# Where the transpose of dt·u and the diagonal scalings stand in their queues: a Mamba block with a quantised feed-forward on one Trainium2 core

## The chip, the cores and the metric

The kernel runs on one core of a Trainium2 chip. The metric is the device time of one execution in microseconds (us). The core's engines work from queues of their own and meet through semaphores: PE (TensorE, matrix products and transposes), DVE (VectorE), ACT (ScalarE), POOL (GpSimd) and SP, which issues the DMAs. Each engine takes its instructions strictly in the order in which they were written, and one that waits holds up all behind it.

## The reference, cut to what matters

```python
x = x + tanh(g_x) * mamba(ctx, z=layernorm(x))      # 4 batches, 512 positions, 512 channels, 16 states
x = x + tanh(g_f) * ffn(layernorm(x))               # 512 -> 2048 -> 512, weights ternary, activations in 8 bits
# mamba, per batch: u = silu(conv(ctx @ w_in)); dt = softplus(...); B, C from u @ w_xp
#   state[n] = state[n] * exp(dt * A[n]) + (dt * u) * B[n];   y += state[n] * C[n]      (n = 0..15, along 512 positions)
#   y = (y + D * u) * silu(z)
# ffn: bitlinear(silu(bitlinear(x, w_gate)) * bitlinear(x, w_up), w_down); bitlinear divides by an rms norm,
#   rounds each row to 8 bits, and multiplies by weights rounded to -1, 0, 1
```

## The kernel before, in words

After a first part (convolution, projections, statistics), the work is cut into 16 stages, one for each batch and each 128 channels (batch `s // 4`, channel block `s % 4`). A stage `s` does the 16 state recurrences of its block: ACT makes `exp(dt * A[n])` into one of three PSUM banks (`exponential`, L1090), DVE runs the scan of state `n` (`scan`, L1428), and the states are then multiplied by C, by DVE (`times_c`, L1450, states 2, 3, 6, 7, 10, 14, 15), or by POOL (L833 for four pairs, L847 for state 11, called `alone`). PE transposes each product and adds it up in PSUM (`y_sum`, `y_sum_pooled`, `y_sum_alone`). The term `(dt * u) * B[n]` comes from POOL (L838), but from stage 5 (`PE_FROM`) on, for states 4 and 5, from PE: `du_transpose` (L515) transposes `dt * u` into the bank `pT` by four 128x128 transposes, ACT's `copy_duT` (L1120) takes it to SBUF, and `db_state` (L522) multiplies it by diagonal matrices that hold B of the two states at each position. ACT writes these diagonals once for a batch, by eight instructions `diagonal(b, i, k)` (L1125): state `i` of the two, block `k` of the positions.

From stage 4 on each stage also does the feed-forward of one token tile `t1 = s - 4` (gate, up, silu) and ends that of an earlier one (`t2 = s - 5`: maximum, scale, transposes; the down product in pieces called `fill`). At its four first tiles of a batch (`t1 % 4 == 0`, stages 4, 8, 12) the tile's statistics are made within the stage, which makes these stages longer.

The order on each engine is written out by hand, and ACT's goes by steps `n = 0..15`. At step `n` of stage `s` ACT makes the exponential of state `n + 2` (at steps 14 and 15 those of states 0 and 1 of the next stage), and after it what else belongs to the step: n = 0 `squares(t2)` (L1056); n = 1 `skip`; n = 2 `scale_x` (L1037); n = 3 sums of the next tile; n = 4 `copy_xqT` (L1043), which waits for PE's transpose of the quantised tile (L546); n = 5, 6 `scale_h`; n = 7, 8 `copy_hqT`; n = 11 the four `gate_silu` (L1048) with the loads of another activation table before and after them; n = 14 `z_copy` (L1108), which takes `pT` to SBUF; n = 15 `copy_duT(s + 1)`. The exponential of a state may run when the scan three states before it is done.

PE ends a stage with `up(t1, 2)`, `du_transpose(s + 1)`, `up(t1, 3)`, `y_sum_alone`, `y_sum(s, 14)`, `c_bcast(s, 15)` (L472, which spreads C of state 15 to all partitions for DVE's `times_c`), and begins the next one with `y_sum(s - 1, 15)`. `y_sum_alone` waits for POOL's L850, `y_sum(s, 15)` for DVE's product L1456 of state 15. DVE's order at that turn is: scan of state 0 of the new stage, `times_c` of state 15, scan 1, scan 2, `gated_y` (L1462), scan 3. "Turn" below is this passage from one stage to the next.

Of the kernel before, what the change touches and what calls it, by code (L numbers as in the profile page):

```python
# [19 lines left out]
NT = D // P  # L20
UNITS = BATCH * NT
# [31 lines left out]
PE_FROM = PLAIN + 1  # L53
# [8 lines left out]
def own(s):  # L62
    return [n for n in range(NS) if n // CH not in pooled(s) and not alone(s, n)]
# [18 lines left out]
def pool_pairs(s):  # L82
    return [c for c in range(NCH) if s < PE_FROM or c != PE_PAIR]
# [5 lines left out]
def db_count(s, c):  # L89

    return DB_AT[s] + pool_pairs(s).index(c) + 1


def by_pe(s, n):
# [19 lines left out]
def past(eng, sem, value):  # L114

    if value > 0:
        eng.wait_ge(sem, value)
# [7 lines left out]
def build(nc, x, ctxT, g_x, g_f, w_in, w_conv, b_conv, w_xp, w_dt, b_dt, a_log, d_skip, w_gate, w_up, w_down,  # L125
          bc_rows, u_rows, out):
    with ExitStack() as stack:
# [267 lines left out]
        def _(pe):  # L395
# [76 lines left out]
            def c_bcast(s, n):  # L472
                m = own(s).index(n)

                past(pe, S["s_mul"], OWN_AT[s] + m - (1 if s < PLAIN else 0))
                for k in range(NT):
                    mm = pe.transpose(c_bank(s, m)[:, k * P:(k + 1) * P],  # L477
                                      xdT[:, s // NT, k, NS + n:NS + n + 1].to_broadcast([P, P]), ident[:, :])
                mm.then_inc(S["s_cb"], 1)
# [7 lines left out]
            def y_sum(s, n):  # L487
                m = own(s).index(n)
                if m == 0:
                    past(pe, S["s_y"], s)  # L490
                pe.wait_ge(S["s_mul"], OWN_AT[s] + m + 1)
                y_part(p_st[(OWN_AT[s] + m) % NH], first=(m == 0 and s < PLAIN), last=((s < PLAIN or s == UNITS - 1) and n == NS - 1)).then_inc(S["s_ytr"], 1)

            def y_sum_pooled(s, j):
                pe.wait_ge(S["s_pmul"], POOLED_AT[s] + j + 1)
                for i in range(CH):
                    mm = y_part(hp[j][:, i, :], last=(j == 3 and i == CH - 1 and s < UNITS - 1))
                mm.then_inc(S["s_pytr"], 1)
# [16 lines left out]
            def du_transpose(s):  # L515
                pe.wait_ge(S["s_du"], s + 1)
                pe.wait_ge(S["s_szT"], s)
                for k in range(NT):
                    mm = pe.transpose(pT[:, k * P:(k + 1) * P], du[s % 2][:, k * P:(k + 1) * P], ident[:, :])
                mm.then_inc(S["s_dup"], 1)  # L520
# [88 lines left out]
            def fill(s, first, last):  # L609

                for part in range(first, last):
                    if s - NT - 2 >= 0:
                        down(s - NT - 2, part, s)
                    else:
                        keep_on(s)
# [26 lines left out]

            for s in range(PLAIN, UNITS):
                t1, t2 = s - NT, s - NT - 1
                if s > PLAIN:
                    y_sum(s - 1, 15)
                    y_sum_pooled(s - 1, 3)
                c_bcast(s, 2)
                fill(s, 0, 1)
                if s >= PE_FROM:  # L650
                    db_state(s, 0)
                    db_state(s, 1)
                y_skip(s)
                y_sum(s, 2)
                c_bcast(s, 3)
                fill(s, 1, 4)
                if t1 % NT:
                    pe.wait_ge(S["f_h"], FC * t1)
                    xq_transpose(t1, pG[0])
                y_sum(s, 3)  # L660
                c_bcast(s, 6)
                y_sum_pooled(s, 0)
                if t2 >= 0:
                    if t1 % NT:
                        pe.wait_ge(S["f_xqT"], t1 + 1)
                    hq_transpose(t2, 0, pG)
                    hq_transpose(t2, 1, pG)
                fill(s, 4, DPARTS)
                if t2 >= 0:
                    hq_transpose(t2, 2, pG)  # L670
                    hq_transpose(t2, 3, pG)
                y_sum(s, 6)
                c_bcast(s, 7)
                if t1 % NT == 0:
                    past(pe, S["f_h"], FC * t1)
                    past(pe, S["f_hqT"], HR * t1 - 1)
                    xq_transpose(t1, pG[0])
                gate(t1, 0)
                gate(t1, 1)
                if t1 % NT:  # L680
                    y_sum_pooled(s, 1)
                    c_bcast(s, 10)
                    y_sum(s, 7)
                    gate(t1, 2)
                    gate(t1, 3)
                else:

                    c_bcast(s, 10)
                    y_sum(s, 7)
                    y_sum_pooled(s, 1)  # L690
                    gate(t1, 2)
                    if ALONE in own(s):
                        c_bcast(s, ALONE)
                    gate(t1, 3)
                y_sum(s, 10)
                up(t1, 0)
                up(t1, 1)
                z_transpose(s)
                if ALONE in own(s):
                    y_sum(s, ALONE)  # L700
                y_sum_pooled(s, 2)
                c_bcast(s, 14)
                if s < UNITS - 1:
                    up(t1, 2)
                    du_transpose(s + 1)
                    up(t1, 3)
                    if s >= PE_FROM:
                        y_sum_alone(s)
                    y_sum(s, 14)
                    c_bcast(s, 15)  # L710

            s, t = UNITS - 1, UNITS - NT
# [209 lines left out]
        def _(act):  # L922
# [202 lines left out]
            def diagonal(b, i, k):  # L1125

                if b == 1:
                    act.wait_ge(S["s_dbu"], db_count(PE_FROM - 1, PE_PAIR))
                else:
                    act.wait_ge(S["s_dbp"], CH * (b * NT - 1 - PE_FROM) + i + 1)  # L1130
                n = CH * PE_PAIR + i
                act.activation(diag_b[i][:, k, :], ident[:, :], ACT.Copy, scale=xdT[:, b, k, n:n + 1]).then_inc(S["s_diag"], 1)
# [36 lines left out]
            for s in range(PLAIN, UNITS):  # L1169
                t1, t2 = s - NT, s - NT - 1  # L1170
                for n in range(NS):
                    if s * NS + n + 2 < UNITS * NS:
                        exponential(s * NS + n + 2)
                    if n == 0 and t2 >= 0:
                        squares(t2)
                    if n == 1:
                        skip(s)
                    if s == PLAIN and n == 3:

                        w_sign(2, 0)  # L1180
                    if n == (2 if t1 % NT else 7):
                        scale_x(t1)
                    if n == 3 and (t1 + 1) % NT:
                        x_sum(t1 + 1)
                        centre(t1 + 1)
                    if n == 4 and (t1 + 1) % NT:
                        x_deviation(t1 + 1)
                        if t1 % NT:
                            x_variance(t1 + 1)
                    if n in (3, 4) and s % NT == NT - 1 and s + 1 < UNITS:  # L1190

                        for k in range(NT):
                            diagonal(s // NT + 1, n - 3, k)
                    if n == 5 and t1 % NT == 0:
                        centre(t1)
                    if n == (4 if t1 % NT else 9):
                        copy_xqT(t1, pG[0][:, :])
                    if n in (5, 6) and t2 >= 0:
                        scale_h(t2, n - 5)
                    if n == 7 and t1 % NT == 0:  # L1200
                        x_variance(t1 + 1)
                    if n in (7, 8) and t2 >= 0:
                        copy_hqT(t2, 2 * n - 14, pG)
                        copy_hqT(t2, 2 * n - 13, pG)
                    if s == PE_FROM - 1 and n in (2, 4, 6, 8):

                        diagonal(1, n // 6, n - 2 - 4 * (n // 6))
                        diagonal(1, n // 6, n - 1 - 4 * (n // 6))
                    if n == 11:
                        gate_silu(t1, 0, gate_bank(0))  # L1210
                        gate_silu(t1, 1, gate_bank(1))
                        if s + 1 < UNITS:
                            z_silu(s + 1)
                        gate_silu(t1, 2, gate_bank(2))
                        gate_silu(t1, 3, gate_bank(3))
                    if n == 14:
                        z_copy(s)
                    if n == 15 and s + 1 < UNITS:
                        copy_duT(s + 1)
# [371 lines left out]
```

## Time and profile before

| | |
|---|---|
| median of 3 runs | 624.31 us (623.83 to 624.74) |
| the profiled execution | 624.31 us, its span 622.5 us |
| busy: DVE, PE, ACT, POOL | 90%, 84%, 83%, 82% of the span |
| instructions: PE, ACT, DVE, POOL | 3254, 796, 766, 286 |
| mean granted TensorE clock | 0.964 of full speed |

The span runs from the first to the last instruction in the trace; the execution's time has 1.8 us more around it. "Idle before" is the time an engine stood still before an instruction; the releaser named behind it is what ended that wait. A busy share is a mean over the whole span, and it doesn't say which engine another waits for in a given stage.

### The profile page before, as it was taken

Reading aid. Unit: us, or ns where it says so; the run is one execution under the profiler, and the core shown is the slowest. Engines: PE = TensorE matmul, PEld = TensorE weight load, DVE = VectorE, ACT = ScalarE, POOL = GpSimd, SP = SyncE. Lnnn points to the kernel's source line nnn. Section 1 sums busy time; section 2 is a strip of 40 time slices with the busy share of each in tenths; the row PEclk is TensorE's granted clock in tenths of the full one; section 3 lists DMA queues with packets and bytes.
Section 4 is the critical chain, followed back from the end, with each engine's and each line's share of the span. In section 5 each row is a group of like instructions: output and inputs, shape, how many; then the busy total and the mean of one; then the engine's idle time right before and its main releaser. Section 6 shows DMA issues by size and latency. Waiting matters only on the chain. (4 is left out here: it accounts for less than half of the span.)

```text
span 622.5 us, 9751 instructions
## 1 busy us (share of the span) xinstructions
PE 523.0 (84%) x3254; PEld 368.5 (59%) x3254; DVE 557.2 (90%) x766; ACT 516.1 (83%) x796; POOL 508.3 (82%) x286
## 2 busy tenths in 40 slices
PE   6999666857667888989878989898789898999996
PEld 2443355746566767676756666666466666655553
DVE  2899979999999999999999999998999999977564
ACT  4869788885998889898798898987988988778784
POOL 2568799999999799999998999999989999931000
PEclk9999768889888999999999999999999999999999
DMA  8992930710751010118401111175101110000001
GB/s 291 399 414 80 361 138 34 266 56 1 276 200 49 0 53 2 35 35 299 166 27 35 36 34 35 35 262 195 35 35 35 34 35 18 2 17 18 18 18 51
DMA packets 30420, 64.25 MB, mean 103 GB/s; under 512 B 3729, under 2 KB 11921, under 8 KB 27554
## 3 DMA queue, kind: packets, MB, share of 16 engines
q1 hardware_dynamic: 30370, 63.63, 28.9%
q8 instruction: 26, 0.43, 0.3%
q14 instruction: 24, 0.20, 0.1%
HBM read 55.49 MB, written 8.13 MB: 102 GB/s over the span
## 5 line engine op out<-in xcount | busy, mean ns | idle before, releaser
L844 POOL TENSOR_TENSOR area_s<-area_s,b_bc 128x1024 f32<-128x1024 f32 x117 | 275.3, 2363 | 18.3 <-DVE u_all L1448 12.8
L483 PE MATMUL pY<-ident,area_s 128*128 128x128 f32 x532 | 88.6, 292 | 57.2 <-DVE area_s L1456 57.2
L1448 DVE TENSOR_TENSOR_SCAN area_s<-pA,area_s 128x512 f32<-128x512 f32 x88 | 105.1, 1206 | 7.7 <-ACT pA L1101 7.7
L552 PE MATMUL pG<-wq_gu,area_f 128*128 128x512 fp8e4 x448 | 108.1, 379 | 4.1 <-ACT area_f L1046 2.8
L483 PEld LDWEIGHTS pY<-ident,area_s 128*128 128x128 f32 x532 | 62.7, 147 | 75.7 <-DVE area_s L1456 66.7
L836 POOL TENSOR_TENSOR u_all<-u_all 128x1024 f32<-128x1024 f32 x44 | 103.9, 2361 | 0.2 <-DMA u_all<-bc_rows 0.2
L1101 ACT ACTIVATE pA<-dt_all,a_neg 128x512 f32<-128x512 f32 x145 | 97.4, 682 | 6.1 <-DVE area_s L1448 5.7
L1456 DVE TENSOR_TENSOR area_s<-area_s,pC 128x512 f32<-128x512 f32 x133 | 87.8, 663 | 3.0 <-issue 1.3
L477 PE MATMUL pC<-ident,xdT 128*128 128x128 f32 x532 | 83.8, 285 | 1.1 <-ACT dt_all L954 0.7
L552 PEld LDWEIGHTS pG<-wq_gu,area_f 128*128 128x128 bf16 x448 | 41.8, 98 | 47.2 <-ACT area_f L1046 3.9
L477 PEld LDWEIGHTS pC<-ident,xdT 128*128 128x128 f32 x532 | 66.2, 145 | 4.1 <-DVE area_s L1456 2.2
L596 PE MATMUL pT<-wq_dn,area_f 128*128 128x512 fp8e4 x240 | 57.5, 379 | 0.0
L483 PE MATMUL pY<-ident,u_all 128*128 128x128 f32 x352 | 49.4, 287 | 2.0 <-POOL u_all L836 2.0
L483 PEld LDWEIGHTS pY<-ident,u_all 128*128 128x128 f32 x352 | 43.0, 149 | 4.5 <-POOL u_all L836 2.4
L825 POOL TENSOR_TENSOR sm<-sm,neg_half 128x1 f32<-128x1 f32 x16 | 8.9, 559 | 44.9 <-ACT sm L1064 33.7
L1400 DVE TENSOR_TENSOR area_f<-area_f,pG 128x512 f32<-128x512 f32 x52 | 34.3, 677 | 6.5 <-PE pG L552 4.7
L1101 ACT ACTIVATE pC<-dt_all,a_neg 128x512 f32<-128x512 f32 x57 | 39.0, 683 | 1.1 <-DVE u_all L1448 0.6
L1448 DVE TENSOR_TENSOR_SCAN u_all<-pA,area_s 128x512 f32<-128x512 f32 x33 | 39.5, 1211 | 0.1
L583 PE MATMUL pG<-ident,area_f 128*128 128x128 f32 x176 | 24.0, 278 | 18.4 <-ACT area_f L1087 11.5
L1054 ACT ACTIVATE area_f<-pG,sm 128x512 f32<-128x512 f32 x52 | 34.4, 685 | 4.8 <-PE pG L552 3.0
L1448 DVE TENSOR_TENSOR_SCAN area_s<-pC,area_s 128x512 f32<-128x512 f32 x29 | 35.0, 1206 | 2.9 <-ACT pC L1101 2.9
L789 POOL TENSOR_TENSOR area_s<-area_s 128x511 f32<-128x511 f32 x16 | 20.0, 1276 | 20.1 <-DVE area_s L1287 20.1
(211 smaller groups left out, 1148.0 us busy)
## 6 DMA issues: line engine op xcount, KB each, us to landing
b_bc<-bc_rows SPq DMA_DIRECT2D x14, 1024.0 KB, 7.6
area_s<-x SPq DMA_DIRECT2D x32, 256.0 KB, 3.1
u_all<-bc_rows SPq DMA_DIRECT2D x14, 512.0 KB, 6.3
b_bc<-w_gate SPq DMA_DIRECT2D x1, 4096.0 KB, 14.6
dt_all<-x SPq DMA_DIRECT2D x1, 4096.0 KB, 25.0
area_f<-w_up SPq DMA_DIRECT2D x1, 4096.0 KB, 34.3
area_f<-w_down SPq DMA_DIRECT2D x1, 4096.0 KB, 14.5
out<-area_f SPq DMA_DIRECT2D x16, 256.0 KB, 2.0
```

Source lines behind the costliest of these rows:

```text
L477: mm = pe.transpose(c_bank(s, m)[:, k * P:(k + 1) * P], xdT[:, s // NT, k, NS + n:NS + n + 1].to_broadcast([P, P]), ident[:, :])
L483: mm = pe.matmul(pY[:, k * P:(k + 1) * P], src[:, k * P:(k + 1) * P], ident[:, :], is_transpose=True, start=(first and k == 0), stop=(last ...
L552: mm = pe.matmul(bank, xqT[t % 2][:, k, :], wq_gu[:, k, m, c * GW:(c + 1) * GW], start=(k == 0), stop=(k == NT - 1))
L583: mm = pe.transpose(banks[r % 2][:, k * P:(k + 1) * P], h_of(t)[:, (4 * r + k) * P:(4 * r + k + 1) * P], ident[:, :])
L596: mm = pe.matmul(pT[:, :], hqT[t % 2][:, k, :], wq_dn[:, k, :], start=(k == 0), stop=(k == FK - 1))
L836: gp.tensor_tensor(hp[j], hp[j], c_bc[j], ALU.mult).then_inc(S["s_pmul"], 1)
L844: gp.tensor_tensor(db[c % NDB], du[s % 2].rearrange("p (a l) -> p a l", a=1).to_broadcast([P, CH, L]), b_bc[:, CH * c:CH * c + CH, :], ALU ...
L1054: act.activation(h_of(t)[:, c * GW:(c + 1) * GW], bank, ACT.Silu, scale=col(CS[t % 2])).then_inc(S["f_silu"], 1)
L1101: act.activation(exp_bank(s, n), dt_all[:, s, :], ACT.Exp, scale=a_neg[:, s % NT, n:n + 1]).then_inc(S["s_exp"], 1)
L1400: dve.tensor_tensor(chunk, chunk, bank, ALU.mult).then_inc(S["f_h"], 1)
L1448: dve.tensor_tensor_scan(h, at, dbu, 0.0, ALU.mult, ALU.add).then_inc(S["s_scan"], 1)
L1456: dve.tensor_tensor(p_st[i % NH], h_st[i % NH], c_bank(s, m), ALU.mult).then_inc(S["s_mul"], 1)
```

## The change

The four transposes of `dt * u` for stage `s` are issued by PE at the beginning of stage `s`, ahead of `y_sum(s - 1, 15)`, where they were issued between two products (`up(t1, 2)` and `up(t1, 3)`) near the end of stage `s - 1`. The place of ACT's `copy_duT` is not changed. And the eight diagonals of the next batch, which ACT made by fours at steps 3 and 4 of stages 7 and 11 (the last of a batch), are made at steps 3 (two), 4 (two), 5, 6, 9 and 10 (one each), as the last thing of the step. In step 4 that is behind `copy_xqT`. The diagonals of batch 1, made in stage 4, stay.

```diff
+DIAGONAL_AT = {3: ((0, 0), (0, 1)), 4: ((0, 2), (0, 3)), 5: ((1, 0),), 6: ((1, 1),), 9: ((1, 2),), 10: ((1, 3),)}
...
             for s in range(PLAIN, UNITS):
                 t1, t2 = s - NT, s - NT - 1
+                if s >= PE_FROM:
+                    du_transpose(s)
                 if s > PLAIN:
                     y_sum(s - 1, 15)
                     y_sum_pooled(s - 1, 3)
...
                 if s < UNITS - 1:
                     up(t1, 2)
-                    du_transpose(s + 1)
                     up(t1, 3)
...
-                    if n in (3, 4) and s % NT == NT - 1 and s + 1 < UNITS:
-
-                        for k in range(NT):
-                            diagonal(s // NT + 1, n - 3, k)
...
+                    if s % NT == NT - 1 and s + 1 < UNITS and n in DIAGONAL_AT:
+                        for i, k in DIAGONAL_AT[n]:
+                            diagonal(s // NT + 1, i, k)
                     if n == 11:
                         gate_silu(t1, 0, gate_bank(0))
```

## Rows read from the trace of the kernel before

**Rows 1.** The page's busy times: us, share of the span, instructions.
```profile
PE 523.0 (84%) x3254; PEld 368.5 (59%) x3254; DVE 557.2 (90%) x766; ACT 516.1 (83%) x796; POOL 508.3 (82%) x286
```
**Rows 2.** Windows: stretch, its length, busy PE, PEld, DVE, ACT, POOL, clock, DMA, GB/s.
```profile
245.10:275.78 30.68, 27.42 (x194) 20.25 (x193) 29.86 (x40) 26.94 (x46) 30.60 (x17) 1.00 0.12 35
275.78:306.46 30.68, 27.41 (x194) 20.44 (x193) 28.66 (x35) 27.23 (x48) 29.91 (x16) 1.00 0.60 210
```
**Rows 3.** Waits from 200 to 520 us: who for whom; total us, times, longest.
```profile
ACT area_f L1046 <- PE pG L546: 16.1, 8, 2.2
...
DVE area_s L1448 <- ACT pA L1101: 5.0, 7, 1.1
```
**Rows 4.** Timeline, PE and its weight loads, turn 9 to 10: start, us, instruction, idle before.
```profile
364.07 0.63 PE L519 MATMUL pT<-ident,area_s 128*128 128x128 f32 x4
364.53 1.03 PE L552 MATMUL pG<-wq_gu,area_f 128*128 128x512 fp8e4 x4
...
366.30 0.60 PE L477 MATMUL pC<-ident,xdT 128*128 128x128 f32 x4
368.60 0.66 PE L483 MATMUL pY<-ident,area_s 128*128 128x128 f32 x4 [1.70 <-DVE area_s L1456]
...
365.37 0.42 PEld L483 LDWEIGHTS pY<-ident,area_f 128*128 128x128 f32 x4 [0.30 <-POOL area_f L850]
```
**Rows 5.** Timeline, ACT, the same turn.
```profile
364.73 0.60 ACT L1123 ACTIVATE area_s<-pT 128x512 f32<-128x512 f32 x1 [0.23 <-PE pT L519]
...
366.86 1.91 ACT L1060 ACTIVATE area_f<-area_f 128x2048 bf16<-128x2048 f32 x1 [0.95 <-DVE area_f L1400]
...
369.10 0.68 ACT L1101 ACTIVATE pA<-dt_all,a_neg 128x512 f32<-128x512 f32 x1
```
**Rows 6.** Timeline, DVE, the same turn.
```profile
367.88 0.66 DVE L1456 TENSOR_TENSOR area_s<-area_s,pC 128x512 f32<-128x512 f32 x1
...
369.60 1.20 DVE L1448 TENSOR_TENSOR_SCAN area_s<-pC,area_s 128x512 f32<-128x512 f32 x1
...
371.29 1.21 DVE L1448 TENSOR_TENSOR_SCAN area_s<-pA,area_s 128x512 f32<-128x512 f32 x1
```
**Rows 7.** Timeline, ACT, stage 7, from its first diagonals on.
```profile
277.22 1.28 ACT L1132 ACTIVATE b_bc<-ident,xdT 128x128 f32<-128x128 f32 x4
278.40 0.67 ACT L1101 ACTIVATE pA<-dt_all,a_neg 128x512 f32<-128x512 f32 x1
...
282.25 0.60 ACT L1046 ACTIVATE area_f<-pG 128x512 bf16<-128x512 f32 x1 [1.98 <-PE pG L546]
...
291.13 1.28 ACT L1054 ACT_TABLE_LOAD   x1
...
295.15 0.69 ACT L1054 ACTIVATE area_f<-pG,sm 128x512 f32<-128x512 f32 x1 [0.18 <-PE pG L552]
```
**Rows 8.** Timeline, DVE, stage 7, its two waits.
```profile
296.40 0.69 DVE L1400 TENSOR_TENSOR area_f<-area_f,pG 128x512 f32<-128x512 f32 x1 [1.17 <-PE pG L552]
297.88 1.22 DVE L1448 TENSOR_TENSOR_SCAN area_s<-pC,area_s 128x512 f32<-128x512 f32 x1 [0.79 <-ACT pC L1101]
```
**Rows 9.** Timeline, stage 9: ACT's exponential of state 13, DVE's scan of state 10.
```profile
354.66 0.70 ACT L1101 ACTIVATE pA<-dt_all,a_neg 128x512 f32<-128x512 f32 x1
...
353.10 1.20 DVE L1448 TENSOR_TENSOR_SCAN area_s<-pA,area_s 128x512 f32<-128x512 f32 x1
```
**Rows 10.** Timeline, turn 5 to 6: PE's last broadcast of stage 5, scan 3.
```profile
241.01 0.60 PE L477 MATMUL pC<-ident,xdT 128*128 128x128 f32 x4
...
245.68 1.21 DVE L1448 TENSOR_TENSOR_SCAN area_s<-pC,area_s 128x512 f32<-128x512 f32 x1
```
**Rows 11.** Timeline, turn 11 to 12: the same two, and ACT's centring of tile 8.
```profile
427.91 0.60 PE L477 MATMUL pC<-ident,xdT 128*128 128x128 f32 x4
...
432.94 1.21 DVE L1448 TENSOR_TENSOR_SCAN area_s<-pC,area_s 128x512 f32<-128x512 f32 x1
...
440.23 0.72 ACT L1011 ACTIVATE area_f<-dt_all,mv 128x512 f32<-128x512 f32 x1 [1.29 <-DVE mv L1375]
```

## The prediction

> **What bounds the kernel now.** I begin with the busy shares [rows 1]: DVE leads with 90%, and ACT, PE and POOL follow at 82 to 84%. With four engines so close, the shares don't tell which one sets the pace. So I look at one stage, by windows from one `gated_y` to the next [rows 2]. Stage 6 and stage 7 last exactly the same, 30.68 us, though DVE has 29.86 us of work in the one and 28.66 in the other. A stage that keeps its length when DVE loses 1.20 us of work is not DVE-bound.
>
> What it is bound by shows in the waits [rows 3] and two timelines. From 200 to 520 us ACT stands for 16.1 us in front of its copy of PE's transpose (L1046, 8 times, up to 2.2 us), and DVE for 5.0 us in front of scans whose exponential ACT hasn't made. After the 1.98 us wait at 282.25 ACT shows only one more wait, of 0.18 us at 295.15 for PE's gate product [rows 7], until the exponential of state 14, which DVE takes at 297.88 after idling 1.17 and 0.79 us [rows 8]. At the turn of a stage PE idles 1.70 us until DVE has the product of state 15, and then goes on [rows 4]. Put together, this is a ring: DVE from scan 14 to the product of state 15; PE from there to the transpose of the quantised tile; ACT from its copy (step 4) through scale, copies, silus and two table loads to exponential 14; and DVE again. The places with slack are ACT ahead of its L1046 (about 2 us), PE ahead of its L483 (1.70 us), and DVE within the middle of the stage. What is put into slack is free, what is put into the ring is paid in full. I go through the edits by that.
>
> **The transposes on PE.** They leave a place on PE where four of them take 364.53 - 364.07 = 0.46 us [rows 4], and `up(t1, 3)` comes up that much earlier. Nothing gains by it: the `y_sum_alone` behind it waits for POOL's L850 and begins at 365.37, 0.30 us after PE's loads were through [rows 4], so `y_sum(14)` and `c_bcast(15)` stay where they are; and DVE, which reads `up(t1, 3)`, works without a gap from scan 14 to the product at 367.88 [rows 6]. At the new place they start behind `c_bcast(15)`, at 366.30 + 0.46 = 366.76, and end at 367.39, inside PE's idle time, which lasts until 368.60. Cost and gain on PE: 0. They pass no DMA, and POOL's and SP's queues are untouched.
>
> **The wait that this puts on ACT.** `copy_duT` keeps its place in ACT's queue but waits for transposes that now come later. Behind it stand exponential 2 of the new stage, `squares`, exponential 3, `skip`, exponential 4, and so on. Before, the copy started at 364.73, 0.66 after the transposes (364.07) [rows 4, 5]. Now it starts at 366.76 + 0.66 = 367.42, 2.69 us later. Of this, `squares` had an idle time of 0.95 us before it (it waited for DVE), and with the usual overlap of 0.07 between neighbours 1.02 us are taken back: what follows comes 1.67 us later. Exponential 2 stands ahead of `squares`, which moves from 366.86 to 368.53, so it is over by about 368.6, in time for scan 2 at 369.60 [rows 6]. Exponential 3 moves from 369.10 to 370.77, ends at 371.45, and scan 3 can begin at 371.47 instead of 371.29: DVE loses 0.18 us. From the start of the copy to the earliest scan 3 that is 371.47 - 367.42 = 4.05 us. At the turn into stage 6 the broadcast is at 241.01, so scan 3 can begin at 241.01 + 0.46 + 0.66 + 4.05 = 246.18, 0.50 late [rows 10]; at the turn into stage 12, 427.91 + 5.17 = 433.08, 0.14 late [rows 11].
>
> Is DVE's loss paid? In an ordinary stage ACT is given back its 1.67 us at L1046, where it idles 2.2 us at most [rows 3]. DVE's delay reaches ACT only through the banks, and the tightest one that I find is exponential 13, which starts at 354.66 where scan 10 ended at 354.30, so 0.36 us are free, less 0.02 for the signal [rows 9]. 0.18 fits into 0.34, and DVE's idle time before scan 14 becomes shorter by it: cost 0. In stage 6 the delay is 0.50, so 0.16 is paid. In stages 8 and 12 the ring runs another way: ACT waits 1.29 us for DVE's statistics of the tile [rows 11], DVE's work up to them is dense, and the 0.14 is paid in each. The sum of this part is 0.16 + 2 x 0.14 = 0.44 us. If the cover at L1046 were gone, 1.67 us at a turn would be paid.
>
> **The diagonals.** All eight of stage 7 stood ahead of the 1.98 us wait for PE, so ACT gave them from its slack. Four of them and their neighbour take 278.40 - 277.22 = 1.18 us, 0.295 each [rows 7]. Of the new places only the two at step 3 are ahead of the wait. The six others (two at step 4, and one at 5, 6, 9, 10) stand behind `copy_xqT` and ahead of the silus of step 11, in the stretch in which ACT has no idle time. So the silus, the up product, and exponential 14 come 6 x 0.295 = 1.77 us later, and so does the end of the stage. What is taken out ahead of the wait only makes the wait longer. DVE's idle 1.17 and 0.79 us [rows 8] don't help: DVE waits there for this very chain. Twice, in stages 7 and 11: 3.54 us. The trace of before shows no diagonal in the dense stretch, so I bound the price: nothing, if ACT has hidden slack there; 6 x 0.386 = 2.32 us for a stage, if neighbours don't overlap (386 ns is the median of one of them: 1.28 - 3 x 0.295 gives the same). I take 0.295, because the rows at 277.22 and 278.40 are the same instruction beside an exponential. DVE's own stall of 0.18 in these two stages disappears behind the longer chain.
>
> What does the Trainium skill make of it? Its page "Perfetto Trace Analysis", section Identifying the Most-Contended Engine, names the engine with the highest occupancy as the bottleneck. Here that would be DVE, and diagonals on ACT would be free as long as DVE has work. The equal stages above speak against it; it is the page's side of rival A below.
>
> **The sum.** 624.31 (the profiled execution, which is also the median of the three runs) + 3.54 + 0.44 = 628.3 us, slower by 0.64%.
>
> **Rivals.**
> A. The diagonals are hidden. Mechanism: DVE sets the pace of stages 7 and 11, and its 1.17 + 0.79 = 1.96 us of idle time, more than 1.77, takes up ACT's delay. For it: DVE's busy share [rows 1], and that ACT works only 27.23 of the 30.68 us of stage 7 [rows 2]. Against it: both idle times end by ACT's chain. Time: 624.31 + 0.44 = 624.75, no change.
> B. DVE's late scan 3 is paid at every turn, because DVE, dense in the first two thirds of a stage, is on the ring in ordinary stages too. It decides where exponential 13 has less than 0.18 us in hand. For it: POOL is busy for 30.60 of 30.68 us in stage 6 [rows 2], so little can be made good. Against it: the 0.36 us in stage 9 and DVE's idle time before scan 14. Eleven turns: 10 x 0.18 + 0.50 = 2.30; time 624.31 + 3.54 + 2.30 = 630.2.
> C. The turn runs through PE's queue, so that taking the transposes from in front of `up(t1, 3)` shortens every stage. It decides where `c_bcast(15)` ends later than DVE could begin the product of state 15; then a turn gains 0.46 us, and the stall of scan 3 falls away with it. 11 x 0.46 = 5.06 against 3.54: 622.8, faster. For it: PE has 84% and has no idle time named in front of these instructions other than POOL's 0.30. Against it: `c_bcast(15)` is done at 366.90, and DVE takes it at 367.88 [rows 4, 6].
>
> **How the numbers follow.** A measurement of this kernel can tell about 0.2%, 1.25 us, from no change. Forecast 0.70 (its own range 627.2 to 629.4: the price of a diagonal between 0.2 and 0.386), A 0.13, B 0.12, C 0.05. The predicted time is the forecast's, 628.3. The range runs from 625.7, which takes in a part-hidden set of diagonals (half of 3.54 hidden gives 626.5) but not A and C, to 630.2, which holds B and the upper price of the diagonals (624.31 + 4.64 + 0.44 = 629.4); outside it lie 0.18. Slower: 0.70 + 0.12 = 0.82; same: A, 0.13; faster: C, 0.05.
>
> **What would show it.** In the trace of the changed kernel: (1) ACT waits about 2.6 us for L519 at each of ten or eleven turns, where it waited 0.23; (2) PE's idle time at L483 falls from 1.70 to about 1.2, with the same start; (3) a wait of DVE for ACT of 0.1 to 0.2 us appears at scan 3, 0.5 in stage 6; (4) ordinary stages keep 30.68 us, stages 8 and 12 last about 33.7, stages 7 and 11 about 32.5; (5) in stage 7 ACT's table load comes 1.8 us later after its L1046 than before (8.88 us before). Ordinary stages longer than 30.8 would show B, stages 7 and 11 at 30.7 A, and ordinary stages of 30.2 C. The prediction would be wrong in its sign if the ring didn't pass through ACT's stretch from step 4 to 11.

## The result, and the profile after

| | before | after |
|---|---|---|
| median of 10 runs | 624.13 us (622.81 to 626.33) | 628.29 us (626.87 to 630.0) |
| ratio | | 1.0064, 95% interval 1.005 to 1.0079 |
| the profiled execution, its span | 624.31, 622.5 us | 627.36, 625.5 us |

The change makes the kernel slower by 0.64%, 4.0 us. The prediction was 628.3 us. The busy times on the page of the changed kernel are nearly those of [rows 1]; nothing in them tells that 4 us were lost:

```profile
PE 524.5 (84%) x3254; PEld 367.4 (59%) x3254; DVE 558.1 (89%) x766; ACT 514.9 (82%) x796; POOL 508.3 (81%) x286
```

In code after the change L550 is the transpose that was L546, L1051 `copy_xqT` (L1046), L1128 `copy_duT` (L1123), L523 the transposes of dt·u (L519), L1106 the exponential (L1101), L1404 the product with up (L1400), L1452 the scan (L1448), L1059 the silu (L1054), L1137 a diagonal (L1132).

The windows by stage show the place. They are cut at `gated_y`, as [rows 2] are; the columns are length, busy PE, PEld, DVE, ACT, POOL, clock, DMA share, GB/s. Of the changed kernel stages 6, 7, 8, 9 and 11:

```profile
244.54:275.33 30.79, 27.97 (x194) 20.31 (x193) 29.96 (x40) 26.92 (x45) 30.31 (x17) 1.00 0.11 35
275.33:307.76 32.43, 27.63 (x194) 20.41 (x193) 28.97 (x36) 27.39 (x49) 30.23 (x16) 1.00 0.63 214
307.76:341.33 33.57, 27.71 (x194) 20.30 (x193) 32.25 (x49) 27.56 (x46) 30.87 (x18) 1.00 0.11 39
...
341.33:372.01 30.68, 27.58 (x194) 20.28 (x193) 29.86 (x40) 26.73 (x45) 30.23 (x17) 1.00 0.10 35
...
402.69:435.39 32.70, 27.73 (x194) 20.34 (x193) 28.97 (x35) 27.21 (x48) 30.04 (x16) 1.00 0.63 216
```

And of the kernel before stages 8 and 11, which weren't shown yet:

```profile
306.46:340.03 33.57, 27.59 (x194) 20.35 (x193) 32.25 (x49) 27.65 (x47) 30.86 (x18) 1.00 0.16 53
401.39:432.35 30.96, 27.42 (x194) 20.39 (x193) 28.65 (x35) 27.23 (x48) 29.91 (x16) 1.00 0.62 208
```

Stage 7 lasts 1.75 us longer (30.68 before), stage 11 1.74, stage 6 0.11, and every other stage from 5 on within 0.02 of what it was. ACT's work in stages 7 and 11 is the same within 0.2 us. These stages got longer because the same work stands elsewhere. ACT's timeline of stage 7 in the changed kernel shows it:

```profile
278.58 0.68 ACT L1137 ACTIVATE b_bc<-ident,xdT 128x128 f32<-128x128 f32 x2
279.16 0.67 ACT L1106 ACTIVATE pA<-dt_all,a_neg 128x512 f32<-128x512 f32 x1
281.81 0.60 ACT L1051 ACTIVATE area_f<-pG 128x512 bf16<-128x512 f32 x1 [1.98 <-PE pG L550]
282.30 0.68 ACT L1137 ACTIVATE b_bc<-ident,xdT 128x128 f32<-128x128 f32 x2
...
291.43 0.40 ACT L1137 ACTIVATE b_bc<-ident,xdT 128x128 f32<-128x128 f32 x1
291.72 0.69 ACT L1106 ACTIVATE pA<-dt_all,a_neg 128x512 f32<-128x512 f32 x1
292.42 1.28 ACT L1059 ACT_TABLE_LOAD   x1
```

From `copy_xqT` to the table load are 292.42 - 281.81 = 10.61 us, where they were 291.13 - 282.25 = 8.88 [rows 7]: six diagonals, 1.73 us. The silus, the up product and exponential 14 follow. DVE's two waits [rows 8] are still there, the first 0.60 us longer. Ahead of them stand three new ones: at scan 3, which comes from the other edit, and at scans 10 and 11, which wait for exponentials that ACT makes later:

```profile
276.35 1.22 DVE L1452 TENSOR_TENSOR_SCAN area_s<-pA,area_s 128x512 f32<-128x512 f32 x1 [0.35 <-ACT pA L1106]
...
290.64 1.22 DVE L1452 TENSOR_TENSOR_SCAN area_f<-pC,area_s 128x512 f32<-128x512 f32 x1 [0.36 <-ACT pC L1106]
...
297.70 0.69 DVE L1404 TENSOR_TENSOR area_f<-area_f,pG 128x512 f32<-128x512 f32 x1 [1.77 <-PE pG L556]
299.17 1.22 DVE L1452 TENSOR_TENSOR_SCAN area_s<-pC,area_s 128x512 f32<-128x512 f32 x1 [0.79 <-ACT pC L1106]
```

(The wait at scan 10 is too short for a label: it starts 1.31 us after scan 9, at 289.05, where in the kernel before it came 1.11 us after it.) The other edit shows in the waits from 200 to 530 us of the changed kernel, to be read beside [rows 3] (engine and line that waited, for whom; total us, times, longest). ACT now waits for the transposes 11 times, 31.9 us in all (3.1 before). Of these 28.8 us more, 9.2 are saved at `copy_xqT` (6.9 us instead of 16.1), 10.0 at `squares`, where ACT had waited for DVE, and 3.0 at a wait for POOL in stages 8 and 12 (2.3 us instead of 5.3): most of the wait has only moved.

```profile
ACT area_s L1128 <- PE pT L523: 31.9, 11, 3.2
...
ACT area_f L1051 <- PE pG L550: 6.9, 7, 2.2
```

The stages from 4 on sum to 3.6 us more than before, the spans differ by 3.0, the medians by 4.2. Stage 1, which neither edit touches, lasted 25.60 us in this execution and 26.18 in that of before. In the experiments below it is 25.6 or 26.2 us with no relation to the edits, stage 2 lasts 26.5 to 26.9 us and stage 4 32.3 to 32.4, and stage 5 begins anywhere from 213.3 to 216.1 us after the span's start. So single spans are good to about 3 us, and single stages from 5 on to 0.02, but for stages 7 and 11: in one of them, not always the same, a silu waits 0.45 us for PE instead of 0.18 (stage 11 of before: 30.96 against 30.68). One execution of all, of the variant with four diagonals below, took 1449 us; its ratio and time below are without it.

### The profile page after: what moved, and what is told of

Read it like the earlier page. It is cut to its first block and busy times, and to the rows that moved or that the text cites. A ratio compares the mean times of both kernels' runs of the same rounds, so it can differ in the third digit from the quotient of the medians.

```text
span 625.5 us, 9751 instructions
## 1 busy us (share of the span) xinstructions
PE 524.5 (84%) x3254; PEld 367.4 (59%) x3254; DVE 558.1 (89%) x766; ACT 514.9 (82%) x796; POOL 508.3 (81%) x286
## 3 DMA queue, kind: packets, MB, share of 16 engines
HBM read 55.49 MB, written 8.13 MB: 102 GB/s over the span
## 5 line engine op out<-in xcount | busy, mean ns | idle before, releaser
L1452 DVE TENSOR_TENSOR_SCAN area_s<-pA,area_s 128x512 f32<-128x512 f32 x88 | 105.4, 1209 | 8.2 <-ACT pA L1106 6.9
L556 PE MATMUL pG<-wq_gu,area_f 128*128 128x512 fp8e4 x448 | 106.6, 379 | 5.3 <-ACT area_f L1051 2.8
L1106 ACT ACTIVATE pA<-dt_all,a_neg 128x512 f32<-128x512 f32 x145 | 97.4, 681 | 6.4 <-DVE area_s L1452 6.0
L1404 DVE TENSOR_TENSOR area_f<-area_f,pG 128x512 f32<-128x512 f32 x52 | 34.3, 677 | 7.5 <-PE pG L556 5.7
L1452 DVE TENSOR_TENSOR_SCAN u_all<-pA,area_s 128x512 f32<-128x512 f32 x33 | 39.6, 1212 | 0.1
L1106 ACT ACTIVATE pC<-dt_all,a_neg 128x512 f32<-128x512 f32 x57 | 38.8, 681 | 0.7 <-DVE u_all L1452 0.6
L1059 ACT ACTIVATE area_f<-pG,sm 128x512 f32<-128x512 f32 x52 | 34.4, 685 | 4.7 <-PE pG L556 3.0
L1452 DVE TENSOR_TENSOR_SCAN area_s<-pC,area_s 128x512 f32<-128x512 f32 x29 | 35.1, 1209 | 3.6 <-ACT pC L1106 3.4
```

Of the source, the lines that this page charges most:

```text
L556: mm = pe.matmul(bank, xqT[t % 2][:, k, :], wq_gu[:, k, m, c * GW:(c + 1) * GW], start=(k == 0), stop=(k == NT - 1))
L1059: act.activation(h_of(t)[:, c * GW:(c + 1) * GW], bank, ACT.Silu, scale=col(CS[t % 2])).then_inc(S["f_silu"], 1)
L1106: act.activation(exp_bank(s, n), dt_all[:, s, :], ACT.Exp, scale=a_neg[:, s % NT, n:n + 1]).then_inc(S["s_exp"], 1)
L1404: dve.tensor_tensor(chunk, chunk, bank, ALU.mult).then_inc(S["f_h"], 1)
L1452: dve.tensor_tensor_scan(h, at, dbu, 0.0, ALU.mult, ALU.add).then_inc(S["s_scan"], 1)
```

## The experiments

All ratios are to the kernel before, on the same chip, with 95% intervals. The stages are read from the windows between one `gated_y` and the next in each profile.

**Only the diagonals** (the transposes of dt·u as before). The edit is shown against the changed kernel:

```diff
-                if s >= PE_FROM:
-                    du_transpose(s)
...
                     up(t1, 2)
+                    du_transpose(s + 1)
                     up(t1, 3)
```

> Only the diagonals of stages 7 and 11 are moved (to steps 3, 4, 5, 6, 9, 10), the transposes stay. The ring theory: six diagonals of 0.295 us lie in ACT's stretch between copy_xqT and exponential 14, so stages 7 and 11 last 1.77 us longer each (32.45 and 32.7 us), all others as before, and the time is 3.5 us above before. Rival A (DVE sets the pace and its idle time hides them): all stages as before, no change. A rival on the interplay (the diagonals cost only because ACT is late from the moved transposes): stages 7 and 11 are under 31.5 us here.

627.55 us, ratio 1.0057 (1.0038 to 1.0075), 3.6 us. Windows of stages 7 and 11:

```profile
276.32:308.75 32.43, 27.41 (x194) 20.45 (x193) 28.98 (x36) 27.20 (x48) 29.92 (x16) 1.00 0.62 217
403.68:436.38 32.70, 27.42 (x194) 20.38 (x193) 28.98 (x36) 27.19 (x48) 29.91 (x16) 1.00 0.62 217
```

The same two lengths as in the changed kernel, all other stages as before (30.68 in stage 6). The diagonals alone make the 1.75 us; they don't need ACT to be late. Rival A falls.

**Only the transposes** (the diagonals as before). The edit is shown against the kernel before:

```diff
+                if s >= PE_FROM:
+                    du_transpose(s)
                 if s > PLAIN:
                     y_sum(s - 1, 15)
...
-                    du_transpose(s + 1)
```

> Only the transposes of dt*u are moved, the diagonals stay at steps 3 and 4. The ring theory: ACT waits 2.7 to 3.2 us for them at each of 11 turns but has it back at L1046; scan 3 is up to 0.35 us late and only stage 6 is 0.1 us longer; time 0.1 to 0.4 us above before, not to be told from no change. With the eight diagonals ahead of copy_xqT and ACT 1.7 us late, its wait at L1046 in stages 7 and 11 falls from 1.98 us to about 0.3 us or nothing. Rival B (late scan 3 is paid at every turn): each ordinary stage 0.1 to 0.3 us longer, time 2 us above before. Rival C: 5 us below before.

624.87 us, ratio 1.0012 (1.0000 to 1.0024). Stage 6 lasts 30.82 us and stage 7 30.80, 0.14 and 0.12 more than before; stages 9 to 11 are as before (30.69, 30.69, 30.96), 8 and 12 too (33.57, 33.58). Rival B would have each ordinary stage longer, C each shorter; neither is so. ACT's wait at its L1047 (`copy_xqT`) in stage 7 is down from 1.98 to 0.18 us, as expected: the slack is nearly used up. The two edits' stages add up to 3.49 + 0.26 us, in the changed kernel they give 3.49 + 0.11: stage 7's 0.12 is hidden there behind the diagonals.

**Eight, four, none: how many stand in ACT's stretch.** Three variants of the changed kernel that differ from it in one line (the comments at the end of the lines are put in here).

```diff
-DIAGONAL_AT = {3: ((0, 0), (0, 1)), 4: ((0, 2), (0, 3)), 5: ((1, 0),), 6: ((1, 1),), 9: ((1, 2),), 10: ((1, 3),)}
+DIAGONAL_AT = {4: ((0, 0), (0, 1), (0, 2), (0, 3)), 5: ((1, 0),), 6: ((1, 1),), 9: ((1, 2),), 10: ((1, 3),)}   # eight
+DIAGONAL_AT = {3: ((0, 0), (0, 1), (0, 2), (0, 3)), 5: ((1, 0),), 6: ((1, 1),), 9: ((1, 2),), 10: ((1, 3),)}   # four
+DIAGONAL_AT = {15: tuple((i, k) for i in range(2) for k in range(4))}   # none: all at step 15, ahead of copy_duT
```

> The changed kernel, but all eight diagonals stand behind copy_xqT (four at step 4, one each at 5, 6, 9, 10), two more than in the changed kernel. If each diagonal in that stretch is paid with its 0.295 us: stages 7 and 11 last 8 x 0.295 = 2.36 us longer than before (33.0 and 33.3 us), the time is 4.8 us above before. If the loss has another cause than their number in the stretch (where they end, or the exponentials that they hold up at steps 9 and 10), it stays at the changed kernel's 3.5 us.

> The changed kernel with the two diagonals of step 4 put at step 3, ahead of copy_xqT; four stay behind it (steps 5, 6, 9, 10). If each diagonal behind it is paid with 0.295 us: stages 7 and 11 are 4 x 0.295 = 1.18 us longer than before (31.9 and 32.1 us), time 2.4 us above before.

> The transposes moved, and all eight diagonals at step 15 of stages 7 and 11, ahead of copy_duT. They are as far behind copy_xqT as can be, but no longer in ACT's stretch of the ring: there ACT waits 2.76 us for the transposes anyway. The ring theory: 8 x 0.295 = 2.36 us fit into the wait, stages 7 and 11 last 30.68 and 30.96 us, the time is within 0.5 us of before. Rival (any diagonal behind copy_xqT is paid, because ACT has no slack for the rest of the stage): 2.36 us in each of two stages, 4.8 us above before.

Measured: eight 628.95 us, ratio 1.0081 (1.0062 to 1.01); four 627.07 us, 1.0039 (1.0024 to 1.0055); step 15 625.01 us, 1.0011 (0.9999 to 1.0024). Stages 7 and 11 in windows, first of the one with eight, then with four, then with all at step 15:

```profile
274.68:307.69 33.01, 27.63 (x194) 20.39 (x193) 29.07 (x35) 27.40 (x49) 30.26 (x16) 1.00 0.63 215
402.62:435.90 33.28, 27.73 (x194) 20.34 (x193) 29.07 (x35) 27.20 (x48) 30.06 (x16) 1.00 0.60 214
```
```profile
276.62:308.46 31.84, 27.62 (x194) 20.39 (x193) 28.86 (x36) 27.40 (x49) 30.24 (x16) 1.00 0.58 210
403.40:435.52 32.12, 27.74 (x194) 20.35 (x193) 28.86 (x36) 27.19 (x48) 30.00 (x16) 1.00 0.58 214
```
```profile
276.43:307.50 31.07, 27.99 (x194) 20.23 (x193) 28.74 (x36) 27.52 (x49) 30.25 (x16) 1.00 0.59 203
402.44:433.12 30.68, 27.85 (x194) 20.29 (x193) 28.74 (x35) 27.25 (x48) 30.02 (x16) 1.00 0.59 206
```

Against before (30.68, 30.96) stage 7 is longer by 2.33, 1.75, 1.16 us with eight, six and four diagonals in the stretch: 0.290 to 0.292 us for each of them; stage 11 gives 2.32, 1.74, 1.16. At step 15 the eight are further behind `copy_xqT` than ever, and cost nothing: the two stages sum to 61.75 us against 61.76 with only the transposes moved (in this profile stage 7 is the one with the silu's 0.45 us wait, which is why the pair has to be summed). They run in ACT's wait for the transposes; it is 0.39 us now, down from 2.76:

```profile
301.22 2.44 ACT L1137 ACTIVATE b_bc<-ident,xdT 128x128 f32<-128x128 f32 x8
304.05 0.60 ACT L1128 ACTIVATE area_s<-pT 128x512 f32<-128x512 f32 x1 [0.39 <-PE pT L523]
```

So it isn't how late in the stage a diagonal stands, nor whether it stands alone or beside three others (the variant with eight has four together at step 4), but whether it stands in the part of ACT's queue that the ring goes through.

**The ring, taken by another end.** The kernel before, with neither edit; PE's part is made shorter by nine products, where `t1 % 4` isn't 0.

```diff
-                fill(s, 1, 4)
                 if t1 % NT:
                     pe.wait_ge(S["f_h"], FC * t1)
                     xq_transpose(t1, pG[0])
+                fill(s, 1, 4)
```

> The kernel before, with one thing changed that neither edit touches: in stages with t1 % 4 != 0 PE makes the transpose of the quantised tile ahead of the nine down products (fill 1 to 4), not behind them. The ring theory: PE's part of the ring gets 1.94 us shorter, ACT's 2.2 us wait at L1046 nearly goes, and the stages shrink until the next engine stops them: DVE, with 0.65 us of idle time in an ordinary stage, or POOL, busy for 29.9 to 30.6 of 30.68 us. So ordinary stages of 30.1 to 30.5 us, stages 7 and 11 of 29.9 to 30.2, and a time 2 to 6 us below before. The rival (DVE or POOL sets the pace already, the ring is a story): stages keep 30.68 us and the time doesn't change, while the wait at L1046 only moves elsewhere.

622.09 us against 624.77, ratio 0.9954 (0.9936 to 0.9972): 2.9 us faster than before, the fastest of all kernels here. Windows of stages 6, 7 and 11:

```profile
243.67:274.02 30.35, 27.60 (x194) 20.27 (x193) 29.87 (x41) 27.32 (x46) 30.27 (x17) 1.00 0.10 35
274.02:304.37 30.35, 27.41 (x194) 20.35 (x193) 28.66 (x36) 27.62 (x47) 30.25 (x16) 1.00 0.61 209
...
398.62:429.25 30.63, 27.42 (x194) 20.30 (x193) 28.66 (x36) 27.62 (x48) 30.25 (x16) 1.00 0.57 207
```

Stages 6, 7, 9, 10, 11, 13 and 14 are 0.33 or 0.34 us shorter each, with the same work. So PE's part, up to its transpose, was on the path that set the pace before. The rival, that DVE or POOL sets it, falls. Of the two POOL is the stronger: it is busy for 30.60 and 29.91 of the 30.68 us of stages 6 and 7, longer than DVE [rows 2]. I had expected DVE or POOL to stop the gain; in stage 7 it is again a ring, with DVE in PE's place. POOL is busy for 30.25 of the 30.35 us there, but from `gated_y` to the next DVE shows only two waits, 0.84 us for PE's up product and 0.79 for exponential 14, and none for POOL. This is read from the rows; what comes next if that ring is shortened wasn't tried. ACT no longer waits at `copy_xqT` but for scan 4 and for DVE's scales, and the latter opens its dense stretch:

```profile
278.54 0.60 ACT L1046 ACTIVATE area_f<-pG 128x512 bf16<-128x512 f32 x1
279.75 0.69 ACT L1101 ACTIVATE pA<-dt_all,a_neg 128x512 f32<-128x512 f32 x1 [0.61 <-DVE u_all L1448]
280.90 1.15 ACT L1082 ACTIVATE area_f<-area_f,sm 128x1024 f32<-128x1024 f32 x1 [0.46 <-DVE sm L1417]
282.15 0.69 ACT L1101 ACTIVATE pC<-dt_all,a_neg 128x512 f32<-128x512 f32 x1
```

**The early transpose and the moved diagonals together.** The edit above and that of the diagonals.

> The transpose of the quantised tile ahead of the down products (stages of 30.35 us), and in addition the six diagonals moved behind copy_xqT as in the change. In the early version ACT no longer waits for PE at L1046 in stage 7; it waits 0.61 us for scan 4 before exponential 7 and 0.46 us for DVE's scales before scale_h, so that the ring enters ACT at scale_h of step 5. If a diagonal costs by where it stands to the ring's entry, the two at step 4 are now free and the four at 5, 6, 9, 10 cost 4 x 0.291 = 1.16 us: stages 7 and 11 of 31.5 and 31.8 us, time 2.3 us above the early version and 0.5 us below before. If a diagonal behind copy_xqT costs by itself, they are 1.75 us longer (32.1 and 32.4 us), time 3.5 us above the early version.

623.84 us, ratio 0.9984 (0.9968 to 1.0001). Stages 7 and 11 last 31.16 and 31.43 us, 0.81 and 0.80 longer than with the early transpose alone. Here I missed by a third: not 1.75 (a diagonal behind `copy_xqT` costs by itself), but not 1.16 either. The two at step 4 are free, as expected: `scale_h` starts 6.89 us after `gated_y`, as without them (6.88). The four behind it add 8.94 - 8.13 = 0.81 us from `scale_h` to the table load. The rest of the 1.16 seems to have gone into gaps too short for a label: without the diagonals, exponential 8 stood 282.15 - 280.90 = 1.25 us behind `scale_h` (rows above), 0.20 more than the 1.05 after which the next instruction follows `scale_h` when nothing holds it up, because it waited for scan 5; and exponentials 12 and 13 together took 1.45 us instead of the 1.31 of the kernel before. If the diagonals fill these gaps, 1.16 - 0.20 - 0.14 = 0.82 are left, which agrees; this account was made after the result and not tried.

**Where the transposes' small loss comes from.** Only the transposes moved, as above, and beside this `copy_duT` put off until exponential 3 is made:

```diff
                     if n == 1:
+                        if s >= PE_FROM:
+                            copy_duT(s)
                         skip(s)
...
-                    if n == 15 and s + 1 < UNITS:
-                        copy_duT(s + 1)
```

> The transposes moved (diagonals as before), and ACT's copy_duT moved behind exponential 3, to step 1 of the new stage. If the 0.12 to 0.14 us that stages 6 and 7 lost with the transposes alone came through ACT's wait (POOL's product of state 11, PE's queue, the transposes, the copy, exponential 3, scan 3), then DVE no longer waits at scan 3, the wait of 2.8 to 3.2 us for the transposes is gone, and stages 6 and 7 are back at 30.68 us. If the loss comes from the transposes' new place on PE, it stays at 30.8 us. The time is within 0.3 us of before.

625.12 us, ratio 1.0004 (0.9986 to 1.0022). ACT's wait for the transposes is gone, DVE doesn't wait at scan 3, and stages 6 and 7 last 30.72 and 30.71 us instead of 30.82 and 30.80. So 0.09 to 0.10 us of the 0.12 to 0.14 came through ACT's wait. All ordinary stages last 0.02 to 0.04 us more than before in this version; why, I haven't tried.

## Why the prediction was right, by its own steps

- **What bounds the kernel: right, and shown for two of its three parts.** The ring was read from rows, and experiments now bear out two parts of it: work put on ACT's part, from `copy_xqT` to the silus, is paid in full (0.291 us a diagonal in three doses), and work taken from PE's part, ahead of its transpose, is gained until the next ring. DVE's part, from scan 14 to the product of state 15, was changed by no experiment; it rests on the rows. Naming the busiest engine would have put the diagonals at nothing. The rule that the prediction cited from the Trainium skill (Perfetto Trace Analysis, Identifying the Most-Contended Engine) doesn't hold for these stages. DVE leads in occupancy over the whole span (90%), but 1.20 us less of its work in stage 7 than in stage 6 didn't shorten the stage, and ACT's order lengthened it. The prediction overlooked that within stages 6 and 7 POOL leads (30.60 and 29.91 us against DVE's 29.86 and 28.66 [rows 2]), and its rivals have no case in which POOL sets the pace. The early transpose of the quantised tile answers that case too: it shortened both stages by 0.33 us.
- **The diagonals: right.** 0.295 us each was forecast, 0.291 measured, 3.49 instead of 3.54 us for both stages. (The check of the upper price in the prediction is off: 1.28 - 3 x 0.295 is 0.395, not 0.386. Only the range used the upper price.)
- **The transposes on PE: no cost, right.** They lie in PE's idle time at the turn from stage 9 to 10: PE's wait for the product of state 15 falls from 1.70 to 1.27 us, about 1.2 forecast, and ends at the same distance from `gated_y` (2.10 us ahead of it, 2.11 before). My reason why `up(t1, 3)` gains nothing by it (that POOL's L850 holds up `y_sum_alone`) was taken from the turn 9 to 10 and holds there. At the turns 7 to 8 and 11 to 12 of the changed kernel it doesn't: PE shows no wait for POOL there and waits 0.24 us for DVE's product of state 14.
- **ACT's wait: right in kind, and better in the working than in the sign.** The list of signs says about 2.6 us, but the working gives 0.23 + 2.69 = 2.92 for the turn from 9 to 10. There are 2.88 there, and 2.76 to 3.20 over all turns. As worked out, ACT has part of it back at `squares` and the rest at `copy_xqT`.
- **The 0.44 us of this part: mis-sized.** It was to be 0.16 in stage 6 and 0.14 each in stages 8 and 12. Measured: 0.11, 0.00 and 0.01. The estimate of 5.17 us from `c_bcast(15)` to scan 3 was too long. At the turn into stage 8 of the changed kernel the transposes start 0.44 us behind the broadcast (I had 0.46), the copy 0.64 us later (0.66), scan 3 4.03 us behind it (4.05), 5.11 in all; and the broadcast comes 0.09 us earlier before `gated_y` (4.53 us against 4.44), because PE no longer has the transposes ahead of it. Scan 3 is just in time.
- **Scan 3 in other stages: the picture was too simple.** I forecast 0.18 late at every ordinary turn. In the changed kernel it stands 0.58 us behind `gated_y` in stages 8, 9, 12 and 13 (no delay), 0.70 in 10, 0.81 in 11, and 1.02 in 6 and 7. From stage 9 to 11 it grows by 0.11 or 0.12 us a stage. The starts of `copy_duT` at the turns into 9, 10 and 11 (337.88, 368.68, 399.47) lie 30.80 and 30.79 us apart, not 30.68:

```profile
337.88 0.60 ACT L1128 ACTIVATE area_s<-pT 128x512 f32<-128x512 f32 x1 [2.76 <-PE pT L523]
```
```profile
368.68 0.60 ACT L1128 ACTIVATE area_s<-pT 128x512 f32<-128x512 f32 x1 [2.88 <-PE pT L523]
```
```profile
399.47 0.60 ACT L1128 ACTIVATE area_s<-pT 128x512 f32<-128x512 f32 x1 [2.98 <-PE pT L523]
```

  A second ring has come into being: POOL's product for state 11, `y_sum_alone`, `c_bcast(15)`, the transposes, `copy_duT`, exponential 3, scan 3 and the scans behind it, and POOL's next product with B, which waits 0.39 us for DVE in stage 10 (0.37 in stage 9, where scan 3 isn't late):

```profile
380.38 2.36 POOL L849 TENSOR_TENSOR area_s<-area_s,b_bc 128x1024 f32<-128x1024 f32 x1 [0.39 <-DVE u_all L1452]
```

  It runs 0.11 us slower than the first, whose slack of 0.34 us [rows 9] hides it for some stages; in stage 6 scan 3 is 0.44 us late, the slack is used up, and the 0.11 us are paid. Stages 8 and 12 are long and set it back. That ACT's wait carries the delay to DVE is shown by the experiment with the late copy: there scan 3 is 0.58 or 0.59 us behind `gated_y` in every stage. That POOL closes this ring and gives the 30.79 us is only argued: POOL's product for state 11 comes 30.81 us later in stage 10 than in stage 9, in step with the copies, but its wait for DVE grows by just 0.02 us, and no run changed POOL's part.
- **The sum.** 3.49 + 0.11 = 3.60 us by stages, 3.98 forecast, 4.0 (3.1 to 4.9) measured by the ratio. That the median of 628.29 meets 628.3 so closely is partly luck.

## What to carry to other kernels

With several engines at 80 to 90%, look for stages that have equal lengths with unequal work, and follow one stage round by its waits. Slack ahead of an engine's wait says nothing of slack behind it: ACT had 2 us ahead of `copy_xqT` in stage 7 and almost none from there to exponential 14. An instruction's price is set by where it stands to the ring: eight small ones ahead of the 2 us wait were free, four, six or eight of them behind it were paid to the last, and eight in the next wait, at the stage's end, were free again. Before a transfer between engines is moved behind another engine's work, ask which new ring it closes, and whether it is slower than the old one.

## What the runs showed of the hardware that was not expected

Nothing of the hardware itself was unexpected. Each diagonal in ACT's dense stretch made the stage 0.290 to 0.292 us longer in every dose, though the trace records 0.386 us for one of them (the median): it overlaps with its neighbour. The granted clock of PE was 1.00 in each of the stages compared.
